# Score stacks copied inside SBUF from dimension-major tiles to rows eight partitions apart, with one fill of ones in place of two fills

## The reference

```python
q = hidden @ Wq.T; k = hidden @ Wk.T; v = hidden @ Wv.T
q = q * cos + rotate_half(q) * sin            # angle of column c: position / 10000 ** (2 * (c % 128) / 256)
k = k * cos + rotate_half(k) * sin
q, k, v = split_heads(q), split_heads(k), split_heads(v)    # 16 heads of 16 columns: head h has columns 16h .. 16h+15
k_feat, q_feat = elu(k) + 1, elu(q) + 1
memory = einsum('bhsd,bhse->bhde', k_feat, v)               # linear attention, per head
mem_out = einsum('bhsd,bhde->bhse', q_feat, memory) / einsum('bhsd,bhd->bhs', q_feat, k_feat.sum(axis=2))
attn = softmax(q @ k.T / sqrt(16)) @ v
combined = sigmoid(gate) * mem_out + (1 - sigmoid(gate)) * attn
x = x + combined @ Wo.T
x = x + (fwht(silu(h @ W1.T) * (h @ W3.T))) @ W2.T          # h = layernorm(x)
```

## Time and profile before

| | |
|---|---|
| median of 3 runs | 251.76 us (251.26 to 253.08) |
| the profiled execution: its time | 254.45 us |
| the profiled execution: span of the trace | 252.6 us |
| TensorE busy | 200.2 us, 79% |
| VectorE busy | 174.9 us, 69% |
| ScalarE busy | 97.8 us, 39% |
| GpSimd busy | 95.7 us, 38% |
| moved by DMA | 17.67 MB; written to outside memory 5.24 MB |
| mean granted TensorE clock | 0.932 of full speed |

### The profile page before, as it was taken

One profiled execution on the slowest core, in us unless ns is written; L12 is line 12 of the kernel. 1 busy time (PEld: TensorE's weight loads), 2 busy tenths in 40 slices (PEclk: granted clock), 3 DMA queues, 4 the chain that ended last, 5 costly groups with the idle time before them and its releaser, 6 DMA issues.

```text
span 252.6 us, 4048 instructions
## 1 busy us (share of the span) xinstructions
PE 200.2 (79%) x1444; PEld 169.1 (67%) x1444; DVE 174.9 (69%) x341; ACT 97.8 (39%) x196; POOL 95.7 (38%) x73
## 2 busy tenths in 40 slices
PE   0064066886897949999999699999879999959894
PEld 0064055873544939997788599877769986748893
DVE  6966862498898597838879967448998562962442
ACT  2261131042884012368810325686021577312231
POOL 7919500069450738323610492152021215111332
PEclk9999655799997997999999899999999999997999
DMA  6919299313087103002790130066800100000101
GB/s 217 384 29 260 86 176 120 38 43 130 0 122 114 22 31 111 31 2 51 79 128 1 43 114 20 4 91 99 109 0 0 49 0 3 1 1 0 44 0 42
DMA packets 16940, 17.67 MB, mean 70 GB/s; under 512 B 1676, under 2 KB 16268, under 8 KB 16908
## 3 DMA queue, kind: packets, MB, share of 16 engines
q1 hardware_dynamic: 16168, 16.68, 31.9%
q10 hardware_dynamic: 752, 0.73, 0.9%
HBM read 11.93 MB, written 5.24 MB: 68 GB/s over the span
## 4 chain that ended last, share of the span: by engine, by line
PE 43%; issue 22%; DVE 17%; POOL 8%; DMA 6%; SPq 2%; ACT 2%; POOLq 0%; DVEq 0%; ACTq 0%
DVE rowmax_pad L628 5%; DMA k_stack<-parts 5%; PE score_bank L901 5%; PE score_bank L1010 4%; PE exp_bank L919 4%; DVE xn L611 4%; PE down_bank L1032 4%; POOL hid_lo L525 4%; PE exp_bank L1010 3%; PE misc_bank L848 2%; DVE prod L639 2%; PE pv_bank L936 2%; PE misc_bank L849 2%; PE misc_bank L850 2%; PE misc_bank L969 2%
## 5 line engine op out<-in xcount | busy, mean ns | idle before, releaser
L628 DVE TENSOR_REDUCE rowmax_pad<-score_bank 128x2 f32<-128x512 f32 x64 | 42.8, 685 | 17.8 <-PE score_bank L901 17.8
L525 POOL TENSOR_TENSOR hid_lo<-wide_raw,hid_hi 128x256 fp32r<-128x256 f32 x32 | 25.0, 782 | 70.6 <-ACT hid_hi L400 67.1
L367 ACT ACTIVATE prob<-exp_bank 128x512 f32<-128x512 f32 x64 | 37.8, 601 | 15.4 <-PE exp_bank L919 15.1
L901 PE MATMUL score_bank<-k_stack,q_stack 128*128 128x256 f32 x128 | 31.1, 337 | 14.7 <-DVE rowmax_pad L628 10.5
L901 PEld LDWEIGHTS score_bank<-k_stack,q_stack 128*128 128x128 f32 x128 | 21.8, 205 | 20.0 <-DVE rowmax_pad L628 10.8
L919 PE MATMUL exp_bank<-q_stack,k_stack 128*128 128x256 f32 x128 | 28.5, 306 | 2.5 <-DMA q_stack<-nmT_lo 1.4
L919 PEld LDWEIGHTS exp_bank<-q_stack,k_stack 128*128 128x128 f32 x128 | 19.2, 189 | 14.0 <-issue 8.2
L506 POOL TENSOR_TENSOR roped<-prod 128x512 f32<-128x512 f32 x6 | 7.6, 1271 | 44.0 <-DVE prod L639 44.0
L738 DVE SCALAR_TENSOR_TENSOR wide_raw<-wide_raw,score_bank 128x256 f32<-128x256 f32 x16 | 6.7, 418 | 23.3 <-ACT wide_raw L394 23.3
L861 PE MATMUL misc_bank<-cst,xn 128*128 128x128 f32 x16 | 3.4, 351 | 23.9 <-DVE xn L611 23.9
L1032 PE MATMUL down_bank<-w_hi,hid_hi 128*128 128x256 f32 x64 | 17.5, 296 | 1.4 <-ACT hid_hi L400 1.4
(11 more groups left out here) (117 smaller groups left out, 547.4 us busy)
## 6 DMA issues: line engine op xcount, KB each, us to landing
q_stack<-parts SPq DMA_DIRECT2D x24, 128.0 KB
k_stack<-parts SPq DMA_DIRECT2D x24, 128.0 KB
parts<-part_hi SPq DMA_DIRECT2D x8, 256.0 KB, 2.2
parts<-part_lo SPq DMA_DIRECT2D x8, 256.0 KB, 2.4
xs<-in_x SPq DMA_DIRECT2D x4, 256.0 KB, 6.6
wide_raw<-in_w1T SPq DMA_DIRECT2D x1, 1024.0 KB, 8.2
wide_raw<-in_w3T SPq DMA_DIRECT2D x1, 1024.0 KB, 10.0
narrow_raw<-in_w2T SPq DMA_DIRECT2D x1, 1024.0 KB, 6.0
```

Source lines behind the costliest of these rows:

```text
L367: act.activation(prob[:, h % 8], exp_bank[h % 2][:], ACT.Exp, scale=SCALE).then_inc(prob_s, 1)
L525: pool.tensor_tensor(hid_lo[:, n % 3, :], ffn_work[n % 3], hid_hi[:, n % 3, :].bitcast(F32), ALU.subtract).then_inc(hid_lo_s, 1)
L628: dve.tensor_reduce(rowmax[:, h, :], score_bank[h % 2][:], AX.X, ALU.max).then_inc(rowmax_s, 1)
L901: mm = pe.matmul(bank[:, tt, :], q_stack[:, h, tt * P:tt * P + P], k_stack[:, h, :], start=True, stop=True)
```

## The change

The columns of Wq and Wk are permuted on the host (`by_dim`), so that inside each half c partition 8d + h holds dimension d of head h: the parts come out dimension-major. The cosine and sine tables and the mask of the linear attention's memory are permuted to match. The scratch tensor and `write_parts` are gone. `load_stacks` copies from `part_hi` and `part_lo` straight to the stacks, six DMAs of 128 KB for each c as before: the source is a whole tile of 128 partitions, the destination 16 rows that lie eight partitions apart, rows 0, 8, ..., 120 for slot 0, rows 4, 12, ... for slot 1 and rows 5, 13, ... for slot 2. MAXROW is 2. The four DMAs that read part_hi are issued first, then the two that read part_lo, each set behind its own semaphore. k_stack is filled with ones by a single memset, so the unused rows of k are ones against zeros in q; the clearing of the two rows of q_stack takes its zeros from a new small tile `zeros`, two partitions of 256 elements, filled by a second, small memset. `split_parts` and `low_parts` now wait for `stack_in` of the batch before, where they waited for `parts_out`.

```diff
-MAXROW = 64
+ROW_STEP = 8
+ROW_AT = (0, 4, 5)
+MAXROW = 2
...
-    c[:, C_MASK:C_MASK + HH] = (i[:, None] // HD == np.arange(HH)[None, :])
+    c[:, C_MASK:C_MASK + HH] = (i[:, None] % HH == np.arange(HH)[None, :])
...
-        parts = nc.dram_tensor("parts", [NB, 2, DC, 2, P, S], F32, kind="Internal").ap()
+        def stack_count(b):
+            return 16 * (6 + 7 * b)
...
-            def write_parts(b, c):
-
-                for half, (t, ready) in enumerate(((part_hi, part_hi_s), (part_lo, part_lo_s))):
-                    sp.wait_ge(ready, DC * b + c + 1)
-                    sp.dma_start(parts[b, half, c].rearrange("m p n -> p m n"), t[:, c].bitcast(F32)).then_inc(parts_out[c], 16)
-
             def load_stacks(b, c):
 
-                sp.wait_ge(parts_out[c], 32 * (b + 1))
                 if b == 0:
                     sp.wait_ge(stack_zero, 2)
                 else:
+                    if b == 1 and c == 0:
+                        sp.wait_ge(zeros_set, 1)
                     sp.wait_ge(exp_ps, NH * (b - 1) + HH * (c + 1))
                     sp.dma_start(q_stack[MAXROW:MAXROW + 2, HH * c:HH * c + HH, :].bitcast(F32),
-                                 k_stack[MAXROW + 2:MAXROW + 4, HH * c:HH * c + HH, :].bitcast(F32)).then_inc(stack_in[c], 16)
-                for m, stack, slots in ((0, q_stack, (0, 1, 0)), (1, k_stack, (0, 0, 1))):
-                    for s, half in enumerate(slots):
-                        sp.dma_start(stack[HD * s:HD * s + HD, HH * c:HH * c + HH, :].bitcast(F32),
-                                     parts[b, half, c, m].rearrange("(h d) n -> d h n", d=HD)).then_inc(stack_in[c], 16)
+                                 zeros[:].unsqueeze(1).broadcast_to([2, HH, S])).then_inc(stack_in[c], 16)
+                for src, ready, slots in ((part_hi, part_hi_s, ((0, 0), (0, 2), (1, 0), (1, 1))),
+                                          (part_lo, part_lo_s, ((0, 1), (1, 2)))):
+                    sp.wait_ge(ready, DC * b + c + 1)
+                    for m, s in slots:
+                        sp.dma_start((q_stack, k_stack)[m][ROW_AT[s]:P:ROW_STEP, HH * c:HH * c + HH, :].bitcast(F32),
+                                     src[:, c, m, :].bitcast(F32)).then_inc(stack_in[c], 16)
...
             for r in ROUNDS:
-                if has(r + 1):
-                    for c in range(DC):
-                        write_parts(r + 1, c)
...
             def split_parts(b, c):
                 act.wait_ge(rope_sum, DC * b + c + 1)
                 if b >= 1:
-                    act.wait_ge(parts_out[c], 32 * b)
+                    act.wait_ge(stack_in[c], stack_count(b - 1))
...
                     pool.wait_ge(part_hi_s, DC * b + c + 1)
-                    pool.wait_ge(parts_out[c], 32 * b)
+                    pool.wait_ge(stack_in[c], stack_count(b - 1))
...
-            pool.memset(k_stack[:].bitcast(F32), 0.0).then_inc(k_zero, 1)
-            pool.wait_ge(k_zero, 1)
-            pool.memset(k_stack[MAXROW:MAXROW + 2].bitcast(F32), 1.0).then_inc(stack_zero, 1)
-            pool.wait_ge(stack_zero, 2)
+            pool.memset(k_stack[:].bitcast(F32), 1.0).then_inc(stack_zero, 1)
+            pool.memset(zeros[:], 0.0).then_inc(zeros_set, 1)
...
+    def by_dim(w):
+        return np.ascontiguousarray(np.asarray(w).T.reshape(D, DC, HH, HD).transpose(0, 1, 3, 2).reshape(D, D))
```

More of the change, by code:

```diff
@@ L74, in shape_constants @@
     inv_freq = (1.0 / np.float32(10000.0) ** (np.arange(0, D, 2, dtype=np.float32) / np.float32(D))).astype(np.float32)
+    inv_freq = inv_freq.reshape(HH, HD).T.reshape(P)
     angle = inv_freq[:, None] * np.arange(S, dtype=np.float32)[None, :]
@@ L127, in build @@
         wo = sb("wo", [P, NG, D])
+        zeros = sb("zeros", [2, S])
         stats = sb("stats", [P, TT, 6])
@@ L169, in build @@
         w13_in = [sem("w1_in"), sem("w3_in")]
[L170 removed]
+        (const_in, w2_in, wo_in, gate_in, pad_zero, mhalf_set, wo_zero, stack_zero, zeros_set, v_const, mem_zero, wqkv_hi_s, wqkv_lo_s, w13_hi_s, w1_lo_s, w3_lo_s,
          had_ps, had_sb, fly, w2_hi_s, w2_lo_s, gate_exp, gate_s) = [sem(n) for n in (
[L172 removed]
+             "const_in w2_in wo_in gate_in pad_zero mhalf_set wo_zero stack_zero zeros_set v_const mem_zero wqkv_hi_s wqkv_lo_s w13_hi_s w1_lo_s w3_lo_s "
              "had_ps had_sb fly w2_hi_s w2_lo_s gate_exp gate_s").split()]
@@ L179, in build @@
              "kfT_sb mem_ps mem_sb lin_ps lin_sb").split()]
-        parts_out = [sem("parts_out0"), sem("parts_out1")]
         stack_in = [sem("stack_in0"), sem("stack_in1")]
@@ L299, in _ @@
             sp.wait_ge(y_out, 16 * TT * NB)
-            for c in range(DC):
-                sp.wait_ge(parts_out[c], 32 * NB)
         @block.scalar
@@ L897, in scores @@
                     if h % HH == 0:
-                        pe.wait_ge(stack_in[h // HH], 112 * b + 96)
+                        pe.wait_ge(stack_in[h // HH], stack_count(b))
                     bank = claim(score_bank[h % 2])
@@ L1140 @@
         "x": np.ascontiguousarray(L0_attn_hidden_states),
-        "wqT": turned(L0_attn_Wq), "wkT": turned(L0_attn_Wk), "wvT": turned(L0_attn_Wv), "woT": turned(L0_attn_Wo),
+        "wqT": by_dim(L0_attn_Wq), "wkT": by_dim(L0_attn_Wk), "wvT": turned(L0_attn_Wv), "woT": turned(L0_attn_Wo),
         "gate": gates,
```

2 lines of the change are left out of this document (removed).

## The result

| | before | after |
|---|---|---|
| median of the runs taken together | 252.42 us (251.26 to 254.45, 4 runs) | 243.62 us (240.88 to 244.91, 4 runs) |
| ratio to before, 95% interval | | 0.963 (0.957 to 0.969) |
| the profiled execution: time | 254.45 us | 243.03 us |
| the profiled execution: span, mean granted clock | 252.6 us, 0.932 | 241.2 us, 0.949 |
| moved by DMA; written to outside memory | 17.67 MB; 5.24 MB | 13.47 MB; 1.05 MB |

The changed kernel is 3.7% faster; forecast were 3.8% and 242.2 us. The medians differ by 8.8 us, the two profiled executions by 11.4: the one of before was the longest of its four, and in the one of after the clock rose early at the first scores, as will be seen. So the sum is read from the timed runs, the places from the profiles.

A forecast was written before the change was run, and what follows sets the result against it. Bounds: start-up waits (VectorE held by GpSimd's fills), TensorE's stack waits at batches 0 and 1, and low clock. 3.1 + 2.2 + 1.5 + 2.8 = 9.6 us off, giving 242.2 us from the 251.76 median; range 239.8 to 246.3.

The forecast's parts named there:

- Part 1: Start-up: second long memset becomes short, so VectorE's first normalising pair ends near 9.8 us, not 12.95; -3.1 us.
- Part 2: Batch 0's stacks: without the trip through outside memory, TensorE's 2.22 us wait before the first scores goes whole; -2.2 us.
- Part 3: Behind batch 0's wait: with the gap gone, TensorE's clock can rise sooner; -1.5 us, between nothing and 2.9.
- Part 4: Batch 1's first stacks: copies land at 76.1 us, wait falls to 0.2, clock holds behind the scores; -2.8 us.
- Part 5: New waits of split_parts and low_parts, clearing two rows, SyncE's queue and TensorE's order: all cost nothing.
- Rival (a): Stack copies: spacing brings nothing, copies land at 77.7 us as before; -6.8 us, 245.0 us; chance 0.18.
- Rival (b): First normalising pair: not freed, something else holds VectorE; -6.5 us, 245.3 us; chance 0.07.
- rival (c): Clock rises at once in round 0, holds in round 1, TensorE wins all: 12.0 us, 239.8 us; chance 0.11.
- Rival (d): Stack copies get slower, making batches 1, 2 and 3 late; over 1% slower from +3.1 us per stack; chance 0.04.

The follow-up runs named there:

- one fill alone: Kernel before, with only the single memset of ones over k_stack and the small tile of zeros: 249.91 us, ratio 0.990.
- hold given back: Changed kernel with the small fill put first and a second 4096-element fill directly behind k_stack's: 247.46 us, ratio 0.984 to the kernel before.
- both long fills given back: Two runs, changed kernel plus a second 4096-element fill: behind the small fill, 242.08 us; directly behind k_stack's fill, 247.46 us.
- the fill behind the normalising: Changed kernel with GpSimd's fill of k_stack waiting for both instructions of the first normalising pair: 241.80 us, ratio 0.954 to the kernel before.

## Why the prediction was right, and where it was not

**Part 1, the single fill: right.** Forecast -3.1, measured -2.6 to -3.3 (one fill alone) and 3.4 (hold given back, against the changed kernel beside it). The pair ends at 9.63 (forecast 9.8), the low parts start at 16.13 (16.4), and nothing else was late.

**Part 2, batch 0 without the trip: right in its number and in its ground.** The idle 2.22 us are gone, and the claim that "neither the new rows nor their rate matter here" stands: with neighbouring rows the first scores wait for nothing either. Leaving out the trip is needed for it only in part, as spaced rows with the trip left 0.91 us.

**Part 3, the clock behind batch 0's wait: mis-sized.** I took -1.5 with a bound of -2.9 and had the scores begin at half speed. From ready at 34.36 to the third head's row maximum it was 3.44 us, where before it took 8.28 from ready at 39.38: less the 2.22 of the wait that leaves 2.6 for the clock, and a further 1.7 us had been won ahead of the scores (5.0 - 3.3), which no term held. That is 4.3 in this profile. Its repetition, with the clock rising near 37 us, keeps 1.7 less, so 2.6. With the hold given back and the scores at 38.88, TensorE at the low clock until 42.2, the third head's row maximum came at 43.87, 3.8 us sooner than before and with part 1 taken out, where parts 2 and 3 were forecast at 3.7; less the 2.2 of the wait that is 1.6. So the term lies between 1.6 and 4.3 us against this one profile of before, which was itself a long execution. Its ground, that the clock rises sooner without the gap, is borne out by the profiles side by side. With a wait of 2.2 or 2.5 us ahead of the first scores (the kernel before, the single fill) TensorE stayed at the low clock for 5.9 and 5.3 us from their start. Without a wait it was 1.3 to 3.5 us in six profiles (neighbouring rows, rows two apart, both long fills given back, the changed kernel again, the fill behind the normalising), and in the changed kernel's first profile the clock was up before them. The failing step was to bound a term by the stretch behind the scores, when the rise can fall on either side of them; for the same reason the scores came at 34.36 and 35.44 us in the changed kernel's two profiles, and not at 36.0 to 36.6.

**Part 4, batch 1's first stacks: right in its steps, the sum partly taken back.** The wait is 0.40 us (forecast 0.2, under 0.5), the rate 196 and 197 GB/s once they run (over 150), the clock held behind the scores (16 matmuls in 1.07 us), and from there to batch 2 the kernel wins 11.1 - 8.5 = 2.6 us (2.8). But TensorE was ready 8.5 us sooner and not 9.9, because the clock was low from 56.5 to 59.6 us in the exponentials, where it was high in the profile of before. This I had listed as a danger for the slices after 95 us, not here. Not settled is what puts such a stretch where it falls: it lay at 56 to 60, 57 to 64, and 51 to 57 us in three profiles whose orders on TensorE are alike.

**Part 5: right.** The max row's copies, the new waits and batches 2 and 3 show nothing new, and behind batch 2 the gain is constant.

**Rival (a) was priced wrongly.** It said 245.0 us if the spacing brought nothing, with the copies landing as before. Its test gave 250.92. The step "the copies land at 77.7 as now" failed: a copy that starts inside SBUF and ends in 16 neighbouring rows was slower in all than the load from outside (9.5 us from first issue against 8.0), so it returned at batches 1, 2 and 3 what it won at batch 0. My range would not have held that case. Rival (b) is out by the fill's runs. Of rival (c) only pieces showed: the clock held in round 1. Rival (d), copies slow enough for waits in batches 2 and 3, is the mechanism that the neighbouring rows brought out, at 5.4 us of waits; with spaced rows batches 2 and 3 wait in no profile. Batch 1 waits between nothing and 1.21 us: 0.40 and 0 in the changed kernel's two profiles, 1.21 with the hold given back.

**The sum** of 9.6 us stands against 3.7% and 3.0%, 9.3 and 7.7 us of 252 to 254. Part 1 has its full size in that, so parts 2 to 4 together, forecast at 6.5, were 4.1 (hold given back) to some 6 us. The places in the two profiles add up to more than the runs do (11.4). I put that down to the clock's stretches, which shifted the places by 1 to 2 us between two executions of one kernel, and fell well here; a forecast built from one profile of before took over its long stretches as if they were always there. That the median came within 1.4 us of 242.2 owes something to luck.

## What to carry to other kernels

Look for an instruction that takes several times its twin's duration and lay the other engines' timelines beside it: here GpSimd's long fills and subtractions held small VectorE instructions on the critical path, and moving three of them and two waits was worth 7 us, nearly as much as the whole change. When a DMA lands late, ask first which rows it writes and only then how many trips it makes, since the six copies into rows that are not neighbours took 6.5 us where those into neighbours took 9.5, and the trip saved was worth about 1 us by the waits. A term for the clock should be given the width that it shows between executions of one kernel, and one experiment that takes a single part away is worth more than two profiles compared.

## What the runs showed of the hardware

- **Which VectorE instructions a GpSimd instruction holds.** Beside a fill of 4096 elements a row (3.5 us), two subtract-and-multiply instructions of one tile took 3.96 us instead of 0.73, and 7.40 beside two fills; a subtraction of two tiles ran its 0.67 us in the middle of such a fill. Beside GpSimd's subtraction of two tiles, both kinds were held: 4.21 us for `part_lo` against 0.69, 4.12 and 4.24 for 128x4 elements against 0.16. The Trainium skill, "SBUF — State Buffer", section "🔬 SBUF: two separate sides", says that GpSimd and VectorE share a port pair as an exclusive lock, and that an instruction with two inputs there competes only against a GpSimd instruction that reads. By that rule, the rows of the instructions with two inputs agree: the subtraction beside a fill was free, the one beside GpSimd's subtraction was held.
- **A fill's time** is the same for 2 partitions and 128 (3.54 and 3.51 us).
- **Rows and rates.** Copies of 131 KB inside SBUF: 99 to 137 GB/s into 16 neighbouring rows behind the first microseconds, with a DMA share of 1.08 to 1.20; 189 to 220 into rows two or eight apart, with a share of 0.70 to 0.79. Loads of that size from outside memory into rows eight apart: up to 262 in a microsecond.
- **The time of an issue.** 0.43 us a copy with neighbouring rows from outside memory; about 0.6 when the source is SBUF or the rows are spaced. A copy every 0.63 us is 208 GB/s, and in the changed kernel I take it for what now bounds the copies; no run isolated it. The loads that reached 262 GB/s in single microseconds were issued as slowly and moved 198 on the mean of 64 to 68 us.
- **The clock's rise** near 32.5 and near 37 us in two executions of the same kernel, with VectorE's and GpSimd's rows equal to 0.1 us from 21 to 31.24 us.
